# Attention and LoRA-expert block on one core: maxima of a head pair in halves 4 to 26 of the pair ahead, two buffers for each stack, short pieces in the maxima's banks, x split by other engines

## The reference

```python
x = _layernorm(x + _L0_attn_ref(x, wq, wk, wv, wo))      # x: (4, 1024, 512)
x = _layernorm(x + _L0_ffn_ref(x, A, B, Wr, br))

# attention: 16 heads of 32, no scaling of the scores, no mask
scores = jnp.einsum('bqhd,bkhd->bhqk', xq, xk)
probs = jax.nn.softmax(scores)
out = jnp.einsum('bhqk,bkhd->bqhd', probs, xv).reshape(bsz, seqlen, dim) @ wo.T

# ffn: 8 experts of rank 64, the one with the largest logit is taken
logits = x_flat @ Wr.T + br
probs = jax.nn.softmax(logits, axis=-1)
expert_idx, expert_weight = jnp.argmax(probs, -1), jnp.max(probs, -1)
h = jnp.einsum('nd,erd->ner', x_flat, A)
y = jnp.einsum('ner,eor->neo', h, B) / 64
out = y[token, expert_idx] * expert_weight[:, None]
```

## Time and profile before

| | before |
|---|---|
| time of three runs, us | 1588.32 (1582.56 to 1593.73) |
| time of the profiled execution, us | 1584.57 |
| its span, us | 1582.8 |
| PE busy | 1503.6 us, 95% |
| POOL busy | 1159.1 us, 73% |
| DVE busy | 1008.5 us, 64% |
| ACT busy | 780.5 us, 49% |
| chain that ended last | PE 81%, DVE 9%, issue 3%, DMA 3% |
| mean granted TensorE clock | 0.984 |

### The profile page before, as it was taken

One profiled execution on the slowest core, in us unless ns is written; L12 is line 12 of the kernel. 1 busy time (PEld: TensorE's weight loads), 2 busy tenths in 40 slices (PEclk: granted clock), 3 DMA queues, 4 the chain that ended last, 5 costly groups with the idle time before them and its releaser, 6 DMA issues.

```text
span 1582.8 us, 20393 instructions
## 1 busy us (share of the span) xinstructions
PE 1503.6 (95%) x6856; PEld 845.9 (53%) x6856; DVE 1008.5 (64%) x1764; ACT 780.5 (49%) x1421; POOL 1159.1 (73%) x644
## 2 busy tenths in 40 slices
PE   7699979999999999999998999999999999999998
PEld 5555546666545555556654555555665444453354
DVE  6657676665685767656568667665656777763443
ACT  3245545555454444455545454454554555554332
POOL 0257877999976768777888776778888888889601
PEclk9889989999999999999999999999999999999999
DMA  7244625554423223236342224143633212220001
GB/s 220 60 147 148 200 74 154 151 158 128 118 63 83 61 80 101 68 102 218 99 132 47 68 68 117 51 127 91 198 101 101 48 40 52 52 62 21 8 6 49
DMA packets 80215, 153.12 MB, mean 97 GB/s; under 512 B 19040, under 2 KB 26224, under 8 KB 79728
## 3 DMA queue, kind: packets, MB, share of 16 engines
q1 hardware_dynamic: 78720, 150.24, 33.0%
q0 software_dynamic: 336, 1.07, 0.2%
q10 hardware_dynamic: 1056, 0.52, 0.1%
HBM read 102.52 MB, written 48.49 MB: 95 GB/s over the span
## 4 chain that ended last, share of the span: by engine, by line
PE 81%; DVE 9%; issue 3%; DMA 3%; POOL 2%; SPq 1%; ACT 1%; POOLq 0%; ACTq 0%; DVEq 0%
PE w L621 16%; PE pv L759 14%; PE sc L747 13%; PE mx L737 13%; PE w L700 5%; PE w L687 5%; PE w L656 5%; DVE mxc L960 3%; PE mx L714 2%; DVE xT_s L977 1%; PE w L680 1%; PE w L664 1%; DMA r_f<-wkT 1%; DVE gate L1070 1%; PE mx L700 1%
## 5 line engine op out<-in xcount | busy, mean ns | idle before, releaser
L960 DVE TENSOR_REDUCE mxc<-mx 128x1 f32<-128x512 f32 x1024 | 683.3, 685 | 443.5 <-PE mx L737 441.4
L838 ACT ACTIVATE P<-sc 128x512 f32<-128x512 f32 x1024 | 600.5, 597 | 593.0 <-PE sc L747 574.8
L553 POOL TENSOR_TENSOR Psum<-Psum,P 128x1024 f32<-128x1024 f32 x296 | 701.2, 2397 | 51.0 <-ACT P L838 48.1
L747 PE MATMUL sc<-stack 98*128 98x512 f32 x1024 | 541.3, 531 | 6.7 <-ACT P L838 6.3
L737 PE MATMUL mx<-stack 96*128 96x512 f32 x1024 | 407.3, 403 | 17.8 <-DVE mxc L960 16.0
L747 PEld LDWEIGHTS sc<-stack 98*128 98x128 f32 x1024 | 194.5, 190 | 156.4 <-issue 77.2
L737 PEld LDWEIGHTS mx<-stack 96*128 96x128 f32 x1024 | 196.3, 192 | 127.6 <-issue 60.2
L759 PE MATMUL pv<-P,V 128*32 128x512 f32 x2048 | 262.8, 610 | 0.0
L550 POOL TENSOR_TENSOR Psum<-P 128x1024 f32<-128x1024 f32 x50 | 118.1, 2380 | 152.9 <-PE mx L714 116.0
L621 PE MATMUL w<-xT_s,wqk_s 128*128 128x512 f32 x624 | 199.4, 413 | 21.4 <-DVE xT_s L977 10.3
L621 PEld LDWEIGHTS w<-xT_s,wqk_s 128*128 128x128 f32 x624 | 116.1, 193 | 93.2 <-issue 63.2
(11 more groups left out here) (130 smaller groups left out, 1112.6 us busy)
## 6 DMA issues: line engine op xcount, KB each, us to landing
stack<-qk_parts SPq DMA_DIRECT2D x186, 256.0 KB, 4.3
qk_parts<-split SPq DMA_DIRECT2D x64, 512.0 KB, 3.4
...
```

What stands on the lines that cost most here:

```text
L553: pool.tensor_tensor(sums(s)[:, i, :], sums(s)[:, i, :], P[:, unit % NP, :], ALU.add).then_inc(add_done, 1)
L747: pe.matmul(sc[c][:, :], stack(s, i)[0:KS, 0, 128 * kb:128 * kb + 128], stack(s, i)[0:KS, 1, 512 * c:512 * c + 512], start=True, stop=True ...
L838: act.activation(P[:, unit % NP, 512 * c:512 * c + 512], sc[c][:, :], ACT.Exp).then_inc(exp_done, 1)
L960: dve.tensor_reduce(mxc[:, q % 2, at:at + 1], mx[TURN[g] % NMX][:, :], AX.X, ALU.max).then_inc(mx_done, 1)
```

## The change

- **Maxima.** ITEMS makes all 32 maxima of a pair in halves 4 (FROM_HALF) to 25 of the pair ahead (0 to 25 in pair 0), and none in the ten halves between.
- **Stacks.** `stack0` has two buffers, as `stack1`; both heads of pair s+1 are loaded at half 0 of pair s.
- **Banks.** `t1`, `t2`, `lg` and the new `xi` take turns in the `mx` banks (SHORT, TURNS); a piece three turns behind one waits for ACT's copy of it (t1, t2), for the router's exp (lg), or for the low part of x (xi). The `w` banks are left to the long pieces.
- **Experts.** Another order of pieces: z of the tile before, t2, lg of the next, a share of qk, h of the next, t1 of the one after. P x V blocks always come in twos. The router's bias is added by a product with a row of ones; DVE reads logits in PSUM, the division by the sum moves to the addition of z, and the gate and the biased copy of the logits are gone. Layer norms of z come 11 halves behind z instead of 7.
- **Plan.** Pair 3 has one qk tile instead of two; pairs 4 to 8 are dealt out anew, V tiles 1 to 7 of batch 1 in pair 8, o tiles 0 to 5 in pair 9, o 6 and 7 ahead of the experts.
- **x.** The split for batch 1 (pair 3) passes x through PE by a product with the identity (`xi`), and DVE takes the low part out of PSUM. For batches 2 and 3 POOL makes the low part, one in four halves, from half 10 of pair 9 (17) on.
- **Opening.** The third load of raw weights goes ahead of the stacks of pair 1; slices 4 to 7 are split before the loop.
- **Last pair.** DVE makes every other add (`last_add`).

```diff
-    LEAD = 4
+    FROM_HALF = 4
...
+    SHORT = ("t1", "t2", "lg", "xi")
...
-        pieces = [("t1", at)] + take(0) + [("lg", at), ("h", at), ("t1", at + 1)] + take(1) + [("t2", at)]
+        pieces = [("t1", at)] + take(0) + [("lg", at), ("h", at), ("t1", at + 1)] + take(1)
         for t in range(KB):
-            if t + 1 < KB:
-                pieces += [("lg", at + t + 1), ("h", at + t + 1)]
-            pieces += ([("z", at + t)] if t + 1 < KB else [])
-            if t + 2 < KB:
-                pieces.append(("t1", at + t + 2))
-            if t + 1 < KB:
-                pieces.append(("t2", at + t + 1))
-            pieces += take(t + 2)
+            pieces += ([("z", at + t - 1)] if t else []) + [("t2", at + t)]
+            pieces += ([("lg", at + t + 1)] if t + 1 < KB else []) + take(t + 2)
+            pieces += ([("h", at + t + 1)] if t + 1 < KB else []) + ([("t1", at + t + 2)] if t + 2 < KB else [])
...
-            PLAN[at + 3], FROM[at + 3] = qks(1, 0, 2), 18
-            PLAN[at + 4], PLAN[at + 5], PLAN[at + 6] = qks(1, 2, 5), qks(1, 7, 4), qks(1, 11, 4)
-            PLAN[at + 7] = qks(1, 15, 1) + tiles("v", 1, 0, 4)
+            PLAN[at + 3], FROM[at + 3] = qks(1, 0, 1), 18
+            for n in range(3):
+                PLAN[at + 4 + n] = qks(1, 1 + 4 * n, 4)
+            PLAN[at + 7] = qks(1, 13, 3) + tiles("v", 1, 0, 1)
         else:
-            PLAN[at] = tiles("v", batch, 4, 4) + tiles("o", batch - 1, 0, 2)
-            PLAN[at + 1] = tiles("o", batch - 1, 2, 6)
+            whole = 1 if batch == 1 else 4
+            outputs = tiles("o", batch - 1, 0, KB)
+            first = 0 if batch == 1 else 2
+            PLAN[at] = tiles("v", batch, whole, KB - whole) + outputs[:first]
+            PLAN[at + 1] = outputs[first:6 + first]
             fill = qks(batch + 1, 0, 13) if not final else []
-            for n, pieces in enumerate(spread(expert_pieces(batch - 1, fill), [1] * 5)):
+            for n, pieces in enumerate(spread(outputs[6 + first:] + expert_pieces(batch - 1, fill), [1] * 5)):
...
+    LOAD_X, X_HIGH, X_PASS, X_LOW = {}, {}, {}, {}
+    for batch in range(1, B):
+        at = HALVES * (PAIRS * (batch - 1) + (3 if batch == 1 else 1))
+        for c in range(2):
+            LOAD_X[at + ((1, 9) if batch == 1 else (3, 9))[c]] = batch, c
+        for m in range(2 * KT):
+            place = at + (10 + m + 3 * (m // KT) if batch == 1 else 9 + 4 * m)
+            X_HIGH[place - (batch == 1)] = X_LOW[place + 1] = batch, m
+            if batch == 1:
+                X_PASS[place] = batch, m
...
-        if s < 2:
-            late = 3 * s
-            until = MAXES * (s + 1) + min(MAXES, max(0, MAXES * (h + 1 - late) // (MAX_AT - late)))
-            if s and h >= MAX_AT:
-                until += 2 * (h + 1 - MAX_AT)
-        else:
-            until = half + 1 + MAXES + 2 * LEAD
+        begin = FROM_HALF if s else 0
+        until = MAXES * (s + 1) + min(MAXES, max(0, MAXES * (h + 1 - begin) // (MAX_AT - begin)))
...
-        if s >= PAIRS and 2 <= s % PAIRS < PAIRS - 1:
-            return ((k - 3) // 2,) if k % 2 and k >= 3 else ()
...
+    def next_turn(what):
+        TURN[what], FREES[what] = len(TURNS), frees + (what[0] not in SHORT)
+        TURNS.append(what)
+        return FREES[what]
...
+                    "t2": hmT_done, "lg": lexp_done, "xi": x_lo}
...
+            return (stack0, stack1)[i][:, q % 2, :, :]
...
+            load_raw(2, slice(256, D))
             for i in range(2):
                 load_stack(1, i)
-            load_raw(2, slice(256, D))
...
-                    load_stack(s + 1, 1)
+                    for i in range(2):
+                        load_stack(s + 1, i)
...
-                if h % 2 and 2 <= h // 2 < adds(s) + 2:
+                if h % 2 and 2 <= h // 2 < adds(s) + 2 and (s < LAST or h % 4 == 1):
                     add(s, h // 2)
                     added += 1
+                if half in X_LOW and X_LOW[half][0] > 1:
+                    x_low(*X_LOW[half])
...
+            def take_turn(what):
+
+                turn = TURN[what]
+                if turn >= NMX:
+                    old, n = TURNS[turn - NMX]
+                    if old in SHORT:
+                        pe.wait_ge(FREED_BY[old], n + 1)
+                    else:
+                        pe.wait_ge(mx_done, FREES[old, n])
+                return BANK[what]
...
+                pe.matmul(bank[:, 0:E], one_row[:, :], br_s[0:1, :], start=False, stop=True).then_inc(lg_ready, 1)
...
+            def xi(b, m):
+                c, kt = divmod(m, KT)
+                bank = take_turn(("xi", 2 * KT * b + m))
+                pe.wait_ge(x_loaded[c], 16 * (b + 1))
+                pe.matmul(bank[:, :], ident[:, :], xT_f[:, 1, kt, 512 * c:512 * c + 512], start=True, stop=True).then_inc(xi_ready, 1)
...
-                slice_high(2 + n)
+            slice_high(4)
             copy_max(0)
-            for n in range(6, KB):
-                copy_v(n)
+            slice_high(5)
+            copy_v(6)
+            slice_high(6)
+            copy_v(7)
+            slice_high(7)
...
+                for kind, late in (("o", 7), ("z", 11)):
...
+            def x_low_passed(b, m):
+
+                c, kt = divmod(m, KT)
+                n = 2 * KT * b + m
+                at = slice(512 * c, 512 * c + 512)
+                dve.wait_ge(x_hi, n + 1)
+                dve.wait_ge(xi_ready, n - 2 * KT + 1)
+                dve.tensor_tensor(xT_s[:, 1, kt, at], BANK["xi", n][:, :], xT_s[:, 0, kt, at].bitcast(f32), ALU.subtract).then_inc(x_lo, 1)
...
+            def last_add(k):
+
+                unit = UNITS * LAST + k
+                before = [q for q in range(LAST) if second(q) == second(LAST)]
+                dve.wait_ge(exp_done, 2 * unit + 2)
+                if k == 3:
+                    dve.wait_ge(den_done, before[-1] + 1)
+                    dve.tensor_tensor(sums(LAST)[:, 1, :], P[:, (unit - 2) % NP, :], P[:, unit % NP, :], ALU.add).then_inc(last_added, 1)
+                else:
+                    dve.wait_ge(last_added, k // 2 - 1)
+                    dve.tensor_tensor(sums(LAST)[:, 1, :], sums(LAST)[:, 1, :], P[:, unit % NP, :], ALU.add).then_inc(last_added, 1)
 
...
+                dve.scalar_tensor_tensor(out=eq[:, :], in0=bank[:, 0:E], scalar=lmax[:, :], in1=rank[:, :],
+                                         op0=ALU.is_ge, op1=ALU.mult).then_inc(eq_done, 1)
+                dve.wait_ge(eq_done, n + 1)
+                dve.tensor_reduce(eqm[:, :], eq[:, :], AX.X, ALU.max).then_inc(eqm_done, 1)
...
-            def gates(n):
-                at = 5 * n
...
+                dve.scalar_tensor_tensor(out=res(b)[:, t, :], in0=bank[:, :], scalar=lrec[:, n % 4:n % 4 + 1], in1=res(b)[:, t, :],
+                                         op0=ALU.mult, op1=ALU.add).then_inc(z_added, 1)
...
+            for j in range(4, SLICES):
+                slice_low(j)
```

More of the change, by code:

```diff
@@ L135, in build_attention_lora_moe_block @@
             spent += cost(kind)
-        ORDER += PLAN[s]
+        ORDER += [piece for piece in PLAN[s] if piece[0] not in SHORT]
     ITEMS, made = {}, MAXES
@@ L162, in adds @@
         return UNITS - 2 - 2 * tail(s)
-    ADDS_BEFORE = [sum(adds(q) for q in range(s)) for s in range(SLOTS + 1)]
+    ADDS_BEFORE = [sum(adds(q) // (1 + (q == LAST)) for q in range(s)) for s in range(SLOTS + 1)]
     def den_at(s):
@@ L184, in build_attention_lora_moe_block @@
         for g in ITEMS[half]:
-            TURN[g], turn = turn, turn + 1
+            frees = next_turn(("max", g))
         if h == MAX_AT and s < LAST:
-            TURN["max_t", s + 1], turn = turn, turn + 1
+            frees = next_turn(("max_t", s + 1))
         if s and h == den_at(s):
-            TURN["den", s - 1], turn = turn, turn + 1
-    TURNS = turn
+            frees = next_turn(("den", s - 1))
+        if half in X_PASS:
+            batch, m = X_PASS[half]
+            frees = next_turn(("xi", 2 * KT * batch + m))
+        for kind, n, _ in AT.get(half, ()):
+            if kind in SHORT:
+                frees = next_turn((kind, n))
     FIRST = KB * (B - 1)
@@ L488, in _ @@
                         load_weights(n // 2 + 2)
-                for n in ends(half - 10, "z"):
+                for n in ends(half - 14, "z"):
                     if n % 2:
                         store(n // KB, n % KB - 1)
-                if h == (14 if s else 28) and s + 2 < SLOTS:
-                    sp.wait_ge(sc_ready, half)
-                    load_stack(s + 2, 0)
                 if half % 8 == 6 and half // 8 < SLICES:
@@ L608, in _ @@
         def _(pe):
+            def take_turn(what):
[7 more added lines that the diff above has]
+                return BANK[what]
             def begin(piece, last):
+                if not last and piece[0] in SHORT:
+                    return take_turn(piece)
                 late = BEFORE["last", piece] if last else BEFORE[piece]
@@ L925, in _ @@
```

(17 more changed lines are left out.)

163 lines of the change are left out of this document (83 added, 80 removed).

## The result

The changed kernel takes 1619.47 us (median of four runs, 1617.52 to 1622.85) where the kernel before took 1585.44 beside it: a ratio of 1.0208 (95% interval 1.0162 to 1.0254). It is slower by 1.6 to 2.5%, where 1566 and a gain were forecast.

What follows compares the result with a forecast made beforehand. TensorE was taken as the bound, so only removing its work or stalls pays. The terms summed to -19.2 us, -21 with fewer low-clock stretches, giving 1566 us from 1588.3; range 1545 to 1592.

Steps and rivals of the forecast that it cites:

- Step 1: Opening: reordered loads and copies of V end TensorE's 4.25 us wait and the slow clock behind it, -6 us.
- Step 2: Pair 0: the four slice_low run ahead of the loop, before GpSimd has an add, -7.5 us.
- step 4: Pairs 9 and 17: eight splits leave VectorE for GpSimd, adding 10 to its 39.65 us, -8 us for both.
- step 7: Pair 31: VectorE takes every other add, -5 us; pair 1 loses its early-load wait, -1 us.
- that rival: GpSimd becomes the bound in pairs 9 and 17, layer norms and scores wait: +15 us, 1581, chance 0.08.
- Step 6: Maxima moved to halves 4 to 26: density costs nothing, window ends cost +6.3, +3.7 and +6 us across pairs.
- the three ends: Short pairs: late transpose 1.1 us, shift's landing 0.2, stacks' landing at the window's start 0.3; together 1.6 a pair.
- Step 3: Pair 3: x through TensorE, +6.9 us of work; half of the 16.1 us loss stays because xi banks are held, -8.
- Step 5: Experts: pairs 10 to 14 and 18 to 22 -12 us, pairs 26 to 30 -1, bias products +6.4.
- Step 8: Two o tiles, v tiles and qk tiles only move; the closing stretch neither gains nor loses a stall, 0 us.
- The slower one: Window's ends add up in each of 31 pairs, about 3 us a pair: 46 us more, 1610, chance 0.15.
- The ring rival: Holds in the maxima's three banks eat the experts' gains, each lg costing 2 us, not 1: 1590, chance 0.2.

Runs made afterwards that it cites:

- a2: Changed kernel with the rolling maxima of before (one per half) and three places for a pair's first operands: 1545.44 us, ratio 0.9735.
- a4: Kernel before with only the window (maxima in halves 4 to 26) and two places for first operands, both stacks loaded at half 0: 1655.30 us, ratio 1.0418.
- c1: Changed kernel with VectorE taking the low part of x in the same half as its xi: 1611.12 us, ratio 1.0155.
- c4: Changed kernel with the transpose for the shift in half 27 instead of 26, the window still ending at 26: 1594.87 us, ratio 1.0049.
- a5: Changed kernel, window kept, with three places for first operands, loaded a pair ahead at half 14: 1614.08 us, ratio 1.0162.
- d1: Changed kernel, window kept, with the edits of a5, c4 and c1, load_ab behind the shift's loads, only the first two batches' t1, t2, lg sharing: 1561.99 us.
- c3: b2 with t1, t2 and lg of the third batch in the w banks, plus c1's edit: 1523.51 us, ratio 0.9604.
- a3: Changed kernel, window kept, with t1, t2 and lg back in the two w banks: 1615.15 us, ratio 1.0164.
- b1: b2 with t1, t2 and lg in the two w banks instead of the ring: 1553.39 us, ratio 0.9784.
- b2: a2 with load_ab moved behind the shift's load_max: 1534.26 us, ratio 0.9659.

## Why the prediction was wrong, point by point

Losses in the profiled executions, and what the forecast gave:

| stretch | before | after | a2 | change forecast, steps | change measured |
|---|---|---|---|---|---|
| opening (length) | 63.1 | 56.2 | 55.7 | -6 | -6.8 |
| pair 0 | 14.5 | 5.2 | 3.6 | -7.5 | -9.3 |
| pair 3 | 16.1 | 17.0 | 4.6 | -8 | +0.9 |
| pairs 2, 4 to 7 | 2.0 | 16.8 | 1.5 | about +8 | +14.8 |
| pair 8 | -0.4 | 11.4 | 11.0 | about +2 | +11.8 |
| pairs 9, 17 | 12.0 | 5.5 | 1.4 | -8 | -6.5 |
| pairs 10 to 14, 18 to 22 | 31.9 | 27.0 | 10.3 | -12 | -4.9 |
| pairs 15, 16, 23 to 25 | 0.2 | 6.1 | -0.2 | +6 | +5.9 |
| pairs 26 to 30 | 14.9 | 34.8 | 16.9 | -1 | +19.9 |
| pair 31 | 7.3 | 0.3 | 0.3 | -5 | -7.0 |

The pairs' losses grew by 26.1 (pair 1's 0.5 among them), their work by 12.4, the closing part by 1.3, and the opening fell by 6.8: 33.0, the difference of the two spans.

- **Steps 1, 2, 4 and 7 held.** The opening is under 58; the slice_low take 0.67 to 0.69 each, the last of them 1.35 after the first score; pair 31 lost its 3.40. GpSimd carried the splits of pair 9, so that rival didn't come, but by luck as far as step 4's own sum goes: 10 on top of 39.65 don't fit into 47. It came to 37.09 in 48.8, since only five of the eight splits fell into the pair (6.3 us) and 13 adds stood in it instead of 15, at 2.37 each instead of 2.54. Step 7's second half didn't hold: pair 1 lost 3.6 instead of 3.1 (so it isn't one of the pairs that lose "little more" than 0.1).
- **Step 6 is where the sum broke.** It gave the window 16 us; a2 and a4 measured 74 and 67. Its terms were sound where it had terms: the transpose 1.57 behind its score, +5.9 in pairs 15, 16 and 23 to 25. But it had none for pairs 3, 9 to 14, 17 to 22 and 26 to 30, and there the window costs 51 of its 74 us (after minus a2, 12.4 + 4.1 + 16.7 + 17.9). The sentence at fault is "the density costs nothing there", read off pair 1's maxima. In those 22 halves of pair 1 no xi, lg, t1 or t2 took turns with the maxima, and beside 18.4 us of reduces VectorE had 3.0 of other work (three low parts, a copy of a denominator, a reciprocal). Where VectorE has more in its queue (splits of x and layer norms in a4, the pieces of the ring as well in the changed kernel), a bank is wanted again while VectorE still has something else to make first. In the short pairs the term was 1.6 and the cost is 3.1: the three ends were priced, the denominator's turn at half 10 (0.7) was not.
- **Step 3** left half of the 16.1; 17.0 came. c1 shows the hold itself: one half's delay was worth 8.6. Hold and window are worth more together than apart: without the window, a2 loses 4.6 with the same hold. Its work term, +6.9, was right (pair 3 has 4.1 more work, with a qk tile of 2.8 gone).
- **Step 5** was right that the experts gain, and put the loss in the wrong place: without the window the experts of batches 0 and 1 lose 21.6 less, nearly twice the 12. The window takes 17 of that back, partly by the waits for lexp (10.5 and 2.4 us in the whole kernel), which the forecast had seen, at 1 a tile, without the window's part in them, and by those of the transpose (1.1 in pairs 10 to 14). The bias products and xi came at their price: the pairs hold 12.4 us more work, 6.9 for xi and 5.5 for 24 biases.
- **Step 8** said that V tiles only move. They moved past SyncE's `load_ab`, which waits for the last of them with the shift's loads behind it: 10.1 us. The queue of an engine that only issues was not followed.
- **The rivals.** The slower one (the window's ends cost more, 1610, chance 0.15) is nearest to what came, 1619, but it had the place only half right, so its total owes something to luck. The ends cost about 30 (c4 25, a5 5), and some 27 stay between them when these and the other named places are mended (d1 against c3). The ring rival priced each of 24 lg at 2. In pairs 26 to 30, with 8 lg, sharing the ring cost 10.9 us with the window (a3) and 7.6 without it (b1), 1.4 and 1.0 for each; over the whole kernel the ring brings 19 us without the window (b2 against b1), and nothing with it.

The Trainium skill ("SBUF — State Buffer", Who interferes with whom) was brought in on step 7, and pair 31 of the changed kernel agrees with it:

```profile
1488.24 2.37 POOL L571 TENSOR_TENSOR xT_s_f<-P 128x1024 f32<-128x1024 f32 x1 [1.46 <-ACT P L887]
1489.52 2.18 DVE L1074 TENSOR_TENSOR xT_s_f<-P 128x1024 f32<-128x1024 f32 x1 [1.43 <-ACT P L887]
```

VectorE's add begins inside GpSimd's, which ends at 1490.61; it ends at 1491.70, 1.09 later, as if it had run only from there. The twelve adds took 10.7 and 16.4, and still fit into the 32.3 of the pair. Their sum, 27.1, is above the estimated 21.6, since it counts the time that one add waits for another: VectorE's took 1.23 where it had no such wait.
